# The absolute maximum of each row: ScalarE's Abs and sixteen maxima against four grouped reductions on VectorE

## The reference

```python
scale = cond @ norm_w.T + 1.0
h = x * (scale[:, None, :] * rsqrt(mean(x * x, -1) + 1e-6))
val, gate = split(h @ up_w.T, 2, -1)                  # 2048 columns each
h = val * gelu(gate)
s = 127.0 / clip(max(abs(h), -1), 1e-5, None)         # one per row
hq = clip(round(h * s), -128, 127) / s
x = hq @ weight_quant(down_w).T + x
# second layer: weights that depend on the batch
Wd_b, Wu_b = Wd + 0.1 * (cond @ Wdd.T + bdd), Wu + 0.1 * (cond @ Wdu.T + bdu)
out = x + relu(x @ Wd_b.T + bd) @ Wu_b.T + bu
```

## Time and profile before

| | us |
|---|---|
| median of 3 runs | 993.27 (992.75 to 993.3) |
| the profiled execution | 991.73 |
| its span, first to last instruction | 989.6 |
| TensorE busy | 962.7 (97%) |
| VectorE busy | 649.3 (66%), 1028 instructions |
| ScalarE busy | 444.4 (45%), 823 instructions |
| GpSimd busy | 53.7 (5%) |
| mean granted TensorE clock | 0.992 of full speed |

### The profile page before, as it was taken

The page is one execution under the profiler, slowest core; times in us unless marked ns, Lnnn a source line. Parts: engine busy times, 40 slices in busy tenths (PEclk is TensorE's granted clock), DMA queues, the critical chain, the costliest instruction groups (busy, mean ns, idle before and its releaser), DMA issues.

```text
span 989.6 us, 13640 instructions
## 1 busy us (share of the span) xinstructions
PE 962.7 (97%) x5281; PEld 467.4 (47%) x5311; DVE 649.3 (66%) x1028; ACT 444.4 (45%) x823; POOL 53.7 (5%) x52
## 2 busy tenths in 40 slices
PE   6999989999999999999999999999999999997998
PEld 4555434444444444444444444444444444443553
DVE  5878678756776578656875678566875674338333
ACT  5888557312762257322751266214741265115222
POOL 1000000000000000000000000000000000004254
PEclk9999989999999999999999999999999999999999
DMA  9335443444534443443444434443444434012464
GB/s 329 139 128 167 135 150 114 133 140 122 158 109 129 148 131 115 151 134 109 139 138 138 135 126 124 128 139 113 142 139 118 149 107 117 33 54 86 165 231 178
DMA packets 73305, 134.59 MB, mean 136 GB/s; under 512 B 5268, under 2 KB 10904, under 8 KB 72728
## 3 DMA queue, kind: packets, MB, share of 16 engines
q1 hardware_dynamic: 73240, 133.72, 42.4%
HBM read 112.72 MB, written 20.97 MB: 135 GB/s over the span
## 4 chain that ended last, share of the span: by engine, by line
PE 93%; DVE 3%; DMA 1%; issue 1%; ACT 1%; SPq 0%; POOL 0%; DVEq 0%; POOLq 0%
PE bank L899 22%; PE bank L900 22%; PE bank L901 22%; PE bank L956 11%; PE bank L911 6%; PE bank L1070 3%; PE bank L1055 2%; PE bank L872 1%; PE bank L882 1%; PE bank L1046 1%; DVE h L838 1%; DVE delta_reg L677 1%; DMA delta_reg<-in_L_cond_Wdd 0%; DMA xn<-in_x 0%; PE bank L936 0%
## 5 line engine op out<-in xcount | busy, mean ns | idle before, releaser
L899 PE MATMUL bank<-x_split,w_hi 128*128 128x512 f16 x1024 | 389.8, 381 | 2.2 <-DVE x_split L640 2.2
L900 PE MATMUL bank<-x_split,w_hi 128*128 128x512 f16 x1024 | 389.5, 380 | 0.0
L901 PE MATMUL bank<-x_split,w_lo 128*128 128x512 f16 x1024 | 389.2, 380 | 0.0
L677 DVE STREAM_TRANSPOSE delta_reg<-delta_reg 128x512 f32<-128x512 f32 x256 | 258.8, 1112 | 27.7 <-PE bank L911 22.8
L515 ACT ACTIVATE g<-h 128x512 f32<-128x512 f32 x128 | 80.6, 630 | 306.2 <-DVE h L746 306.2
L899 PEld LDWEIGHTS bank<-x_split,w_hi 128*128 128x128 f16 x1024 | 100.5, 98 | 128.4 <-issue 14.3
L901 PEld LDWEIGHTS bank<-x_split,w_lo 128*128 128x128 f16 x1024 | 100.5, 98 | 121.8 <-issue 1.6
L746 DVE SCALAR_TENSOR_TENSOR h<-bank,desc,g 128x512 f32<-128x512 f32 x128 | 92.6, 723 | 96.4 <-issue 72.0
L900 PEld LDWEIGHTS bank<-x_split,w_hi 128*128 128x128 f16 x1024 | 100.5, 98 | 112.7 <-issue 1.1
L504 ACT ACTIVATE g<-bank,desc 128x512 f32<-128x512 f32 x128 | 87.4, 683 | 124.0 <-PE bank L901 123.8
L956 PE MATMUL bank<-wqT,qreg 128*128 128x512 bf16 x482 | 111.4, 379 | 1.6
(11 more groups left out here) (124 smaller groups left out, 576.9 us busy)
## 6 DMA issues: line engine op xcount, KB each, us to landing
delta_reg<-in_L_cond_Wdd SPq DMA_DIRECT2D x64, 512.0 KB, 3.6
delta_reg<-in_L_cond_Wdu SPq DMA_DIRECT2D x64, 512.0 KB, 3.7
qreg<-in_L_cond_up_w SPq DMA_DIRECT2D x32, 256.0 KB, 4.3
xr<-in_x SPq DMA_DIRECT2D x32, 256.0 KB, 4.3
x_scratch<-xr SPq DMA_DIRECT2D x32, 256.0 KB, 4.7
xn<-in_x SPq DMA_DIRECT2D x7, 1024.0 KB, 6.4
out_y<-w_hi SPq DMA_DIRECT2D x7, 1024.0 KB, 4.3
h<-in_L_cond_down_w SPq DMA_DIRECT2D x4, 1024.0 KB, 7.9
```

The costliest lines, as they stand in the source:

```text
L677: last = dve.transpose(natT[:, t, kk, :, :].rearrange("p a (r e) -> p e a r", e=4), nat[:, u % NAT, kk, :])
L899: pe.matmul(bank[:, :], w_hi[:, k, cols], xh[:, par, k, :], start=(k == 0), stop=False)
L900: pe.matmul(bank[:, :], w_hi[:, k, cols], xl[:, par, k, :], start=False, stop=False)
L901: mm = pe.matmul(bank[:, :], w_lo[:, k, cols], xh[:, par, k, :], start=False, stop=(k == KD - 1))
```

## The change

VectorE no longer reads Abs from g. After tiles 3, 7, 11 and 15 of a chunk it runs one `tensor_reduce` over the four tiles: for each of the 512 rows the maximum of four absolute values, the absolute value being taken inside the instruction. The view given to it has the tile as its innermost dimension, so that neighbouring elements of the read lie 2 KB apart. The first group writes absrun; each later one writes g[:, 1, :] and is followed by a maximum of that and absrun. ScalarE's Abs is gone. Its Gelu now waits for h of tile j − 2, and in every fourth iteration (j % 4 = 1) also until the last group has finished with g[:, 1, :]. `turn_absrun` waits for four groups in place of sixteen tiles.

```diff
@@ ScalarE, run @@
                     if not (first and j < 2):
-                        act.wait_ge(max_done, n - 1)
+                        act.wait_ge(h_done, n - 1)
+                    if j % 4 == 1 and n > 1:
+                        act.wait_ge(max_done, n // 4)
...
-                    act.wait_ge(h_done, n + 1)
-                    act.activation(g[:, j % 2, :], h[:, j, :], ACT.Abs).then_inc(abs_done, 1)
@@ VectorE @@
             def absolute_max(c, j):
-                n = FT * c + j
-                dve.wait_ge(abs_done, n + 1)
-                if j == 0:
-                    dve.tensor_copy(absrun[:, :], g[:, 0, :]).then_inc(max_done, 1)
+                if j % 4 != 3:
+                    return
+                m = 4 * c + j // 4
+                dve.wait_ge(h_done, FT * c + j + 1)
+                tiles = h[:, j - 3:j + 1, :].rearrange("p f t -> p t f")
+                if j == 3:
+                    dve.tensor_reduce(absrun[:, :], tiles, AX.X, ALU.max, apply_absolute_value=True).then_inc(max_done, 1)
                 else:
-                    dve.wait_ge(max_done, n)
-                    dve.tensor_tensor(absrun[:, :], absrun[:, :], g[:, j % 2, :], ALU.max).then_inc(max_done, 1)
+                    if j > 7:
+                        dve.wait_ge(max_done, m)
+                    dve.tensor_reduce(g[:, 1, :], tiles, AX.X, ALU.max, apply_absolute_value=True).then_inc(abs_done, 1)
+                    dve.wait_ge(abs_done, 3 * c + j // 4)
+                    dve.tensor_tensor(absrun[:, :], absrun[:, :], g[:, 1, :], ALU.max).then_inc(max_done, 1)
@@ TensorE @@
             def turn_absrun(c):
-                pe.wait_ge(max_done, FT * (c + 1))
+                pe.wait_ge(max_done, 4 * (c + 1))
```

## The result

The changed kernel takes 1032.33 us (median of 4 runs, 1026.09 to 1033.72) against 993.07 before: a ratio of 1.0383, 95% interval 1.0341 to 1.0426. The prediction was 1025.8 with a range of 1003.5 to 1040. The profiled execution of the changed kernel has a span of 1030.3 us (before 989.6), 40.7 more, and a mean granted clock of 0.978 (before 0.992).

A forecast was written before the change was run, and what follows sets the result against it. TensorE was taken to bound it (93% of the chain); 18.0 + 0.65 + 2.9 + 2.4 − 0.2 + 1.6 + 5.6 + 1.6 = 32.55 us on 991.73 gave 1024.3, plus 1.54 for the median 1025.8; range 1003.5 to 1040.

The forecast's parts named there:

- D: Duration of one new VectorE reduction of 2048 elements per partition: taken as 3.7 us, lower bound 2.35, upper bound 4.45.
- (a): Chunk boundary at turn_absrun, six times: TensorE loses D − 0.7, 3.0 us each, 18.0 in all.
- (b): Groups in iterations 4, 8 and 12 of middle chunks: counted as nothing; last chunk's layer weights up to 1 us late.
- (c): First chunk, where TensorE needs the weights VectorE scaled: iterations 4, 8 and 12 cost 0.65, 2.9 and 2.4 us.
- (d): First chunk from iteration 13: without Abs, L528's pieces and delta loads come 1.3 us earlier; 0.2 us gain left of 2.6.
- (e): Behind the last chunk: h's chain is ready 3.1 us later, 1.5 comes back as steps meet less GpSimd work: 1.6.
- (f): TensorE's clock halved after stops: 1.6 us each; half of seven stops, 5.6, plus 1.6 for one stop over 5 us.
- the first rival: The reduction reads at the full rate, D = 2.35: 13.75 us more, 1007.0 for the median; chance 0.35.
- The third rival: The reduction runs at VectorE's fast rate, 1.3 us: 1.9 us more, 995.2, a gain from D = 1.1 downwards; chance 0.04.

The follow-up runs named there:

- groups of two: The changed kernel with groups of two tiles in place of four, all sixteen tiles reduced: 996.1 us (1.0031 of the kernel before).
- three tiles: The changed kernel with each group reducing only its last three tiles, the first left out: 1002.25 us, run once.
- contiguous: The changed kernel with the reduction's view changed so each group of four is neighbouring words, same element count: 1007.55 us (1.0147 of the kernel before).
- filled wait: The changed kernel with matmuls on constants into an idle bank, put before turn_absrun's wait: 1021.66 us (1.0291 of the kernel before).
- last tiles are single: The changed kernel with tiles 12 to 15 of each chunk back on ScalarE's Abs and single maxima: 1002.56 us (1.0092 of the kernel before).
- old first chunk: The changed kernel with Abs and single maxima kept in the first chunk, the change in chunks 2 to 8 only: 1022.35 us (1.0288 of the kernel before).
- four near streams: The changed kernel with each group reduced by two instructions of 1024 elements, four alternating streams 1 KB apart: 1030.13 us.

## Why the prediction was right, and where its sum was not

**The unknown price.** D was taken from the one row with a stepped operand, 3.7, and is 3.72 in 24 and 3.83 in 8 cases. That is in part luck. The number came out for a reason that the row doesn't give: a 16 byte step on the writing side and four streams on the reading side cost about the same here, while two and three streams, which are stepped as well, cost nearly nothing. With groups of three the same reasoning would have been wrong by 0.9 us. The 0.05 us for each of three starts, taken off 3.8, stands on no row either. (Two small sums of the prediction don't come out: by the figures that the Trainium skill gives on the page "Vector Engine (DVE) Microarchitecture Reference", section "5.2 Measured stream behaviour on trn2", 1.73 ns per column and 75 ns fixed, the estimate is 3.6 us, not 3.7; and the lower end of the range, as described, is 1003.9, not 1003.5.)

**(a) The boundary.** Predicted 3.0 each and 18.0 in all, measured 2.93 each (period 112.10 less 109.17), 17.6. The other kernels give D − 0.71 for what a boundary costs: their periods are 109.69 (groups of two), 110.37 (three tiles), 110.74 (contiguous) and 112.15 (filled wait), less 109.17, for D of 1.23, 1.91, 2.28 and 3.65 to 3.7, and nothing where the last tiles are single. That nothing takes it back held.

**(b) Inside the middle chunks.** Predicted nothing, and so it is (the period of 109.17 with groups in iterations 4, 8 and 12). The last chunk cost 1.0 us more for its layer weights, the up to 1 us that was left to the range.

**(c) The scaled weights of the first chunk.** Predicted 0.65, 2.9 and 2.4. In the timeline of after:

```profile
55.67 1.09 PE L878 MATMUL bank<-identf,qreg 128*128 128x128 f32 x8 [0.35 <-DVE qreg L617]
84.55 1.09 PE L878 MATMUL bank<-identf,qreg 128*128 128x128 f32 x8 [2.55 <-DVE qreg L617]
113.05 1.09 PE L878 MATMUL bank<-identf,qreg 128*128 128x128 f32 x8 [2.29 <-DVE qreg L617]
```

With 0.16 for the modelled ends that is 0.5, 2.7 and 2.45.

**(d) What comes back: the step that failed.** "Without Abs the pieces are rounded earlier, their loads and the first delta loads behind them in SP's queue start 1.3 us earlier, and the transpose that waited 4.87 us for that load starts at 118.7 in place of 120.02." In the changed kernel L528 was free of Abs and stood waiting for its own load instead, and the delta loads were issued no earlier:

```profile
117.19 0.72 ACT L528 ACTIVATE qreg<-qreg,wtot 128x512 f32<-128x512 f32 x1 [2.36 <-DMA qreg<-in_L_cond_down_w]
...
121.41 8.68 SPq L275 DMA_DIRECT2D delta_reg<-in_L_cond_Wdd  x4
...
127.68 2.92 DVE L677 STREAM_TRANSPOSE delta_reg<-delta_reg 128x512 f32<-128x512 f32 x3 [6.80 <-DMA delta_reg<-in_L_cond_Wdd]
```

Measured from the scaled weights of iteration 13 (113.05, before 107.06), the issue is at 8.36 us, before 8.03: 0.3 later, not 1.3 earlier. From the issue to the transposes it then took 6.27 us, before 4.93. From those scaled weights to the transposes of absrun TensorE takes 142.10 − 113.05 = 29.05 us, before 133.69 − 107.06 = 26.63: 2.4 more, where 0.2 less was predicted. That is the 2.6 us which were to come back and didn't. TensorE's wait for the last pieces, whose fall to under 3 was named as a sign, fell to 3.74 only. Why L528's own loads came so late is not shown.

**(e) Behind the last chunk.** The transposes of absrun now wait 4.47 us, before 0.56, 3.9 more where 3.1 more was predicted. The rest is the last maximum: it takes 1.53 us where GpSimd runs beside it, 0.69 at the other boundaries. No kernel was run with GpSimd idle there, so that GpSimd is the cause is read from the overlap.

```profile
931.95 4.17 POOL L432 TENSOR_TENSOR w_hi<-xn,bu_bc 128x512 f32<-128x512 f32 x3
933.47 1.53 DVE L693 TENSOR_TENSOR absrun<-absrun,g 128x512 f32<-128x512 f32 x1
935.05 1.12 PE L942 MATMUL bank<-identf,absrun 128*128 128x128 f32 x4 [4.47 <-DVE absrun L693]
...
936.93 0.17 DVE L647 TENSOR_SCALAR mc<-m 128x4 f32<-128x4 f32 x1
```

What was to come back did: L647 takes 0.17 (before 0.91), and TensorE's wait of 2.08 at `spread_scales` is gone, part of it to a clock at half; with the waits filled, where the clock held, 0.53 of it is left, so 1.55 came back (1.5 predicted).

**(f) The clock, the term that was mis-sized.** The price per fall was right (1.6 predicted, 1.5 measured for 3.5 us). The count was not: "I count half of them, 5.6, and one for the stop of over 5 us", 7.2 us in all. But the clock was down behind four of the six middle stops (257.06, 482.90, 708.60, 823.62), behind the stop at 113.05, and behind those at both ends, and at three of these places (142, 708, 934) for 6.8 us, not 3.5. (The count of seven stops also leaves out the last one, 3.7 by the prediction's own (e).) The trace with filled waits, whose clock holds behind all eight, gives the price: from the first transposes of absrun to the second, on to the seventh, to the eighth and to the end it is shorter than the changed kernel's by 2.9, 5.8, 1.6 and 1.0 us, 11.2 in all.

**The whole sum.** Between the two profiled executions 40.7 us were to be explained and 32.55 were forecast. Of the 8.1 between, 4.0 are the clock (11.2 against 7.2), 2.6 are (d), 1.0 is the last chunk of (b), and 0.7 is (e); (a) and (c) together are within 0.2. Between the forecast and the median it is 6.5, as the forecast adds 1.54 for the median and the changed kernel's median lies at its profiled execution. So the time came within its range with the middle chunks right, one return that didn't come and a clock counted too low, both on the same side. The clock also goes with the spread of the runs, which the kernel before doesn't have: the run of 1026.09 has a mean clock of 0.985, those of 1032 to 1034 0.978.

**The rivals.** The contiguous view took 1007.55 us, near the 1007.0 of the first rival, but in part by luck: its boundaries cost 1.57 each (1.65 predicted), while its first chunk took 4.5 us more, where the rival has 1.05 since it too lets (d) come back, and the fallen clock for which the rival adds 1.6 wasn't there. Its 1.2 for (e) isn't worked out; by the steps of the forecast it would be 0.25. The third rival needed D of about 1.2; with 1.23 (groups of two) the kernel is slower by 0.3%, where the prediction had no change or a gain: here too (d) was to give 2.6 us back, and gave nothing.

## What to carry to other kernels

Grouping operations moves their work to the end of the group, so the last group costs its whole duration wherever something waits for the result: compare that duration with the slack of the one consumer, not the sums of busy time. A stop of TensorE has a second price, the time at half clock behind it, which here was up to as large as the stop and differs from run to run; here matmuls that nobody needs, put into the wait, cost less than it. Before a strided reduction is written, measure it at the real number of alternating streams: here two and three were read at about the rate of a contiguous one, and four took 1.7 times as long an element. And a wait that an edit removes is a gain only if the one behind it isn't as long: an engine freed of one wait may stand at its own load.

## What the runs showed of the hardware

A reduction on VectorE in float32 took, less 140 ns fixed, 1.05 ns an element when contiguous (2281 ns for 2048), 1.06 with two alternating streams (1229 for 1024), 1.15 with three (1909 for 1536), 1.75 with four (3715 for 2048), and 1.76 with four at half the distance (1940 for 1024). Taking the absolute value inside the instruction added nothing that could be seen. A stop of 2.72 us at the same place of the same kernel was followed by a clock at half in four of six cases, by the full clock in two. The kernel with the old first chunk (stops of 2.72 to 3.07) has four of six as well, the one with four near streams (2.91) two of six. At that place stops of 0.30, 0.98 and 1.36 were never followed by it, in 24 cases. From the issue of a load of 512 KB to the first instruction that used it, one and the same first chunk took 4.93 us in one trace and 6.18 in another.
